# Two attentions with routed layers: the first attention's scores as three products of high and low parts, with queries and keys issued ahead and norms moved to GpSimd

## The reference

```python
x = x + attn_a(layernorm(x), w_qkv, w_out, rel_bias)   # 16 heads of 64, bias by relative position
x = x + ffn(layernorm(x), ...)                         # 8 experts, one chosen per token, times its gate
x = x + attn_b(layernorm(x), ...)                      # 16 heads, causal, low-rank keys and values
x = x + ffn(layernorm(x), ...)
```

## Time and profile before

| what | value |
|---|---|
| median of 3 runs | 665.41 us (665.12 to 666.37) |
| the profiled execution | 665.99 us, its span 664.3 us |
| granted TensorE clock, whole span | 1.000 |
| busy share: PE, PEld, DVE, ACT, POOL | 97%, 82%, 71%, 80%, 53% |
| first attention | from about 14 to 290 us |
| second attention | from about 358 to 600 us |
| second-costliest PE group, scores of both attentions (line 605) | 1024 records, 115.2 us busy, 364 ns each |

### The profile page before, as it was taken

The page is one execution under the profiler, slowest core; times in us unless marked ns, Lnnn a source line. Parts: engine busy times, 40 slices in busy tenths (PEclk is TensorE's granted clock), DMA queues, the critical chain, the costliest instruction groups (busy, mean ns, idle before and its releaser), DMA issues. The chain is left out here.

```text
span 664.3 us, 17842 instructions
## 1 busy us (share of the span) xinstructions
PE 645.2 (97%) x5406; PEld 544.9 (82%) x5406; DVE 474.9 (71%) x2147; ACT 533.3 (80%) x1776; POOL 353.9 (53%) x669
## 2 busy tenths in 40 slices
PE   6999999999999999999998999999999999999997
PEld 5778788888888788878997788878888888888997
DVE  4866767777786767988754767687868777898833
ACT  3998888889787878785765999898989898986664
POOL 4654535575546644732116545464757575472647
PEclk9999999999999999999999999999999999999999
DMA  9999989999993000035421000000000000003140
GB/s 265 276 292 283 288 204 320 292 283 288 300 285 93 26 1 2 33 98 163 128 66 41 21 1 1 2 3 9 17 14 9 14 25 2 2 34 99 54 127 21
DMA packets 86844, 74.48 MB, mean 112 GB/s; under 512 B 8001, under 2 KB 83399, under 8 KB 86496
## 3 DMA queue, kind: packets, MB, share of 16 engines
q1 hardware_dynamic: 82288, 66.24, 36.5%
q0 software_dynamic: 2848, 6.33, 3.0%
q10 hardware_dynamic: 1616, 0.79, 0.5%
HBM read 19.93 MB, written 54.00 MB: 111 GB/s over the span
## 5 line engine op out<-in xcount | busy, mean ns | idle before, releaser
L358 POOL TENSOR_SCALAR ring<-ring,rs 128x256 f32<-128x256 f32 (+1 forms) x500 | 218.1, 453 | 206.7 <-DVE rs L1255 206.3
L946 ACT ACTIVATE ring<-ring,mn 128x256 f32<-128x256 f32 (+1 forms) x512 | 243.1, 487 | 1.6 <-DVE mn L1244 1.6
L494 PE MATMUL ps<-ident,ring 128*128 128x128 f32 x896 | 121.1, 275 | 2.7 <-POOL ring L358 1.3
L605 PE MATMUL ps<-qk 64*128 64x256 f32 (+1 forms) x1024 | 115.2, 364 | 0.9 <-DVE mn L1244 0.7
L642 PE MATMUL ps<-pt,v 128*64 128x256 f32 (+1 forms) x1024 | 111.4, 359 | 0.2
L494 PEld LDWEIGHTS ps<-ident,ring 128*128 128x128 f32 x896 | 102.3, 143 | 9.1 <-POOL ring L358 2.5
L946 ACT ACTIVATION_READ_ACCUMULATOR ring<-ring,mn 128x1 f32 x512 | 103.3, 202 | 0.0
L642 PEld LDWEIGHTS ps<-pt,v 128*64 128x64 f32 x1024 | 65.6, 136 | 44.3 <-issue 13.3
L605 PEld LDWEIGHTS ps<-qk 64*128 64x128 f32 x1024 | 82.7, 187 | 18.7 <-issue 9.8
L914 ACT COPY qk<-ps 128x512 f32<-128x512 f32 x128 | 74.7, 583 | 24.1 <-PE ps L491 22.6
L1244 DVE CUSTOM_DVE_ANT_0 ring<-ps,cm 128x128 f32<-128x128 f32 (+1 forms) x256 | 73.8, 351 | 3.5 <-PE ps L605 3.5
(11 more groups left out here) (212 smaller groups left out, 1335.4 us busy)
## 6 DMA issues: line engine op xcount, KB each, us to landing
xs_scratch<-f_ys SPq DMA_DIRECT2D x16, 2064.0 KB, 23.1
yr_scratch<-f_ys SPq DMA_DIRECT2D x8, 1024.0 KB, 10.1
f_xs<-xs_scratch SPq DMA_DIRECT2D x50, 129.0 KB, 2.4
w<-in_W SPq DMA_DIRECT2D x16, 256.0 KB, 5.9
xs_scratch<-f_ys SPq DMA_DIRECT2D x2, 1677.0 KB, 21.2
yr_scratch<-f_ys SPq DMA_DIRECT2D x25, 64.0 KB, 1.5
T<-in_bias SPq DMA_DIRECT2D x2, 512.0 KB, 8.2
T<-in_bias SPq DMA_DIRECT2D x1, 1024.0 KB, 10.8
```

Of the source, the lines that this page charges most:

```text
L358: i = pool.tensor_scalar(ring[:, hh, it, 0:w], ring[:, hh, it, 0:w], rs[:, q], 1.0, ALU.mult, ALU.mult)
L494: return pe.transpose(out, src, ident[:, :])
L605: i = pe.matmul(PS[u % 2][hh][:, 256 * it:256 * it + w], qk[rows, 128 * it:128 * it + 128], qk[rows, 256:256 + w], start=True, stop=True)
L946: i = act.activation(ring[:, hh, it, 0:w], ring[:, hh, it, 0:w], ACT.Exp, bias=mn[:, q], scale=-1.0, accum_out=sm[:, q])
```

## The change

It concerns `st == 0` (the first attention) alone:

- ACT writes the queries and keys of a unit as a rounded high part (`qk_high`, float32r), and DVE, in a new operation `T`, the low part (`qk_low`), PSUM minus high part. Each has two buffers.
- The scores are three products of these parts (`S_three`), two row halves at a time.
- `QK` of an even unit from 2 on is issued in the odd step before it, behind the scores and ahead of `PV`. ACT's copy `T` of it comes between the exponentials of the two heads of unit `s - 2`; DVE's `T` of it comes between the row extremes of units `s - 1` and `s`.
- `(x - mean) * factor` ahead of the attention for sequences 1 to 7 (`pre_a2`) and ahead of gain and bias of the routed layer for sequences 0 to 6 (`post_a2`) is done by GpSimd. DVE waits for these before it overwrites the statistics.

```diff
+def norms_by_pool(st, b):
+    return st == 0 and b > 0
...
+    qk_low = at_first(low_parts, *(sb(f"qkl{i}", [128, 512], F32R, scope=low_parts) for i in range(2)))
...
+    qk_high = at_first(high_parts, *(sb(f"qkh{i}", [128, 512], F32R, scope=high_parts) for i in range(2)))
```

GpSimd:

```diff
+        def norm(dst, src, m, r, done):
+            for j in range(2):
+                i = pool.tensor_scalar(dst[:, j, :], src[:, j, :], m[:, j, 0:1], r[:, j:j + 1], ALU.subtract, ALU.mult)
+            i.then_inc(done, 1)
...
                 pool_pow(rstd, half[:, 0:2], v_var0, p_pow0, B0 + b + 1)
+                if norms_by_pool(st, b):
+                    pool.wait_ge(p_pow0, b + 1)
+                    pool.wait_ge(t_x, b)
+                    norm(a_xh, x[:, 2 * b:2 * b + 2, :], mv, rstd, p_xh)
...
             if (b := post_at(s, "a")) is not None:
-                pool.wait_ge(v_xn, B0 + b + 1)
...
+                if st == 0 and b < NB - 1:
+                    pool.wait_ge(p_pow1, b + 1)
+                    norm(xx, x[:, 2 * b:2 * b + 2, :], m2, r2[:, 2:4], p_set)
+                    set_n[0] += 1
+                    pool.wait_ge(p_set, set_n[0])
+                else:
+                    pool.wait_ge(v_xn, B0 + b + 1 - (NB - 1))
```

TensorE, in `QK` and beside `S`:

```diff
                 pe.wait_ge(a_t, U0 + u)
+                pe.wait_ge(v_t, min(U0 + u, NU))
...
+        def S_three(u):
+            high, low_ = qk_high[u % 2], qk_low[u % 2]
+            pe.wait_ge(a_t, u + 1)
+            pe.wait_ge(v_t, u + 1)
+            for hh, bank in enumerate(((1, 2), (3, 7))[u % 2]):
+                claim(bank, v_mn, 2 * u + hh + 1)
+            for it in range(2):
+                q, k_ = slice(128 * it, 128 * it + 128), slice(256, 512)
+                for n, (a, b) in enumerate(((high, high), (low_, high), (high, low_))):
+                    for hh in range(2):
+                        rows = slice(64 * hh, 64 * hh + 64)
+                        i = pe.matmul(PS[u % 2][hh][:, 256 * it:256 * it + 256], a[rows, q], b[rows, k_],
+                                      start=(n == 0), stop=(n == 2))
+            i.then_inc(t_s, 1)
```

TensorE, in its step:

```diff
-            if 0 <= s < NU:
+            if 0 <= s < NU and not (st == 0 and s and s % 2 == 0):
                 QK(s)
...
                 S(s - 1)
                 S(s)
+                if st == 0 and s + 1 < NU:
+                    QK(s + 1)
```

ACT, in `T`:

```diff
-            act.copy(a_qk[(U0 + u) % 2][:, :], PT_[:, :]).then_inc(a_t, 1)
+            if st == 0:
+                act_high(qk_high[u % 2][:, :], PT_[:, :], a_t)
```

ACT, in its step:

```diff
+            early = st == 0 and s % 2 and 1 <= s < NU - 1
+            if early and s < 2:
+                T(s + 1)
             if 2 <= s < NU + 2:
-                expo(s - 2, (0, 1) if s % 2 or s == NU else (0,))
+                expo(s - 2, (0, 1) if (s % 2 and not early) or s == NU else (0,))
+                if early:
+                    T(s + 1)
+                    expo(s - 2, (1,))
```

DVE:

```diff
+        def T(u):
+            if u >= 2:
+                dve.wait_ge(t_s, u - 1)
+            low(qk_low[u % 2][:, :], PT_[:, :], qk_high[u % 2][:, :], a_t, u + 1, v_t)
...
         def post_a2(b):
+            if st == 0 and b < NB - 1:
+                return
```

DVE, in its step; in an odd step the first addition stands ahead of the update and `TR`, the second between `S(s - 1)` and `S(s)`:

```diff
+            if st == 0 and 0 <= s < NU and (s % 2 or s == 0):
+                T(s)
...
+                if st == 0 and s + 1 < NU:
+                    T(s + 1)
```

More of the change, by code:

```diff
@@ L213, in build, with at_first @@
     f_tok = sb("f_tok", [128, NF], U32)
+    def at_first(scope, *made):
+        scope.close()
+        return made
+    low_parts = ExitStack()
+    qk_low = at_first(low_parts, *(sb(f"qkl{i}", [128, 512], F32R, scope=low_parts) for i in range(2)))
     f_xt = [sb(f"f_xt{i}", [128, 512]) for i in range(2)]
@@ L221, in build @@
     f_sub = sb("f_sub", [128, 4, NE])
-    def at_first(scope, *made):
-        scope.close()
-        return made
     base = ExitStack()
@@ L234, in build @@
     a_pt = [sb(f"pt{i}", [128, 2, 512], scope=base) for i in range(2)]
+    high_parts = ExitStack()
+    qk_high = at_first(high_parts, *(sb(f"qkh{i}", [128, 512], F32R, scope=high_parts) for i in range(2)))
     a_qk = [sb(f"qk{i}", [128, 512], scope=base) for i in range(2)]
@@ L270, in build @@
     p_set, p_nrm, p_xn, p_T = sem("p_set"), sem("p_nrm"), sem("p_xn"), sem("p_T")
-    p_pow0, p_pow1 = sem("p_pow0"), sem("p_pow1")
+    p_pow0, p_pow1, p_xh = sem("p_pow0"), sem("p_pow1"), sem("p_xh")
     t_m, t_wv, t_wo = sem("t_m"), sem("t_wv"), sem("t_wo")
@@ L284, in build @@
     v_m, v_wv, v_wo, v_kd = (sem(n) for n in ("v_m", "v_wv", "v_wo", "v_kd"))
+    v_t = sem("v_t")
     v_x, v_l, v_mn, v_rs, v_nrm, v_pt1, v_o = (
@@ L527, in pre_b @@
             PX = spare(("x", B0 + b), v_x, B0 + b + 1, None if B0 + b else 7)
-            pe.wait_ge(v_xh, B0 + b + 1)
+            if norms_by_pool(st, b):
+                pe.wait_ge(p_xh, b)
+            else:
+                pe.wait_ge(v_xh, b + 2 if st else 1)
             for j in range(2):
@@ L594, in first_queries @@
             three(PT_[:, 0:256], wqkh[:, 0:128], wqkl[:, 0:128], a_xth[0][:, :], a_xtl[0][:, :])
+        def S_three(u):
[12 more added lines that the diff above has]
+            i.then_inc(t_s, 1)
         def S(u):
+            if st == 0:
+                S_three(u)
+                return
             qk = a_qk[(U0 + u) % 2]
@@ L913, in T @@
                 act.wait_ge(t_s, U0 + u - 1)
-            act.copy(a_qk[(U0 + u) % 2][:, :], PT_[:, :]).then_inc(a_t, 1)
+            if st == 0:
+                act_high(qk_high[u % 2][:, :], PT_[:, :], a_t)
+            else:
+                act.copy(a_qk[(U0 + u) % 2][:, :], PT_[:, :]).then_inc(a_t, 1)
         def values(b, n):
@@ L1198, in pre_a @@
         def pre_a(b):
+            if norms_by_pool(st, b - 1):
+                dve.wait_ge(p_xh, b - 1)
+            if st and b == 0:
+                dve.wait_ge(p_xh, NB - 1)
             come = d_yt[2 * b:2 * b + 2] if st else (d_x[min(b, 2)], None)
@@ L1284, in out_last @@
             dve.wait_ge(v_res, B0 + b + 1)
+            if st == 0:
+                dve.wait_ge(p_xn, b)
             norm_a(xx, s2, m2, r2, v_var1)
@@ L1294, in sums @@
             dve.wait_ge(v_res, B0 + b + 1)
+            if st == 0 and b:
+                dve.wait_ge(p_xn, b)
             norm_a(x[:, 2 * b:2 * b + 2, :], s2, m2, r2, v_var1)
```

## The result

The changed kernel takes **688.6 us** (median of 4 runs, 688.46 to 691.57) beside 665.89 us for the kernel before (4 runs, 665.12 to 668.48): a ratio of 1.035 [1.033, 1.038], 22.7 us slower. The sign of the forecast holds, and its mechanism does in the steady pairs; the size does not, above all at the start: 13.8 us were forecast, and 688.6 lies 0.6 beyond the range's upper end, 688 (for the lower end the forecast gives 671 in one place and 660 in another). The profiled execution took 688.62 us.

What follows compares the result with a forecast made beforehand. TensorE bounded the kernel; after the change a path through ACT, DVE and GpSimd would set 8.3 us pairs. Pair, placement and start terms sum to 13.8: 665.99 + 13.8 - 0.6 = 679.2 us, range 671 to 688 (elsewhere 660 to 688).

Steps and rivals of the forecast that it cites:

- The mechanism: First attention pairs: DVE's wait for ACT's copy delays minima, reciprocal, GpSimd's scaling and TensorE's transposes; 8.3 us; chance 0.62.
- TensorE stays the bound: Rival, first attention: the path through the other engines is under some 7.8 us; total about 661 us; chance 0.22.
- The scores: TensorE's score block of a pair takes 1.60 us instead of 1.93, a gain of 0.33, loads side by side.
- rival of serial loads: TensorE's score loads of two row halves do not run side by side; 1.4 us more, 724 in all; chance 0.07.
- The extra change of shape: Moving QK between S and PV adds one change of TensorE's array shape per pair, +0.19 us.
- The sums' pair: Pair with the step of the sums: DVE's update, copy and statistics lengthen the path to 9.0 us instead of 8.3.
- the projection's: Pair holding the output projection: TensorE's own sum, 11.01 us, a change of -0.14, seven times.
- placement: DVE's placement chain stands ahead of the odd unit's low part; TensorE's S(o) waits 1.35 us, three times.
- The plain pairs: Pairs with neither sums nor projection: the path through DVE and GpSimd sums to 8.29, taken as 8.3 us.
- The start: DVE's low parts of units 1 and 2 queue late: 1.8 us (0.7 to 2.5), plus 0.3 for a first pair.
- The end: Last pair of the first attention: +0.6 us, counted with the sums' pairs.
- The norms: Two 128x128 operations per sequence moved from DVE to GpSimd: 0.4 us each, costed at nothing; uncovered, some 8 more.

Runs made afterwards that it cites:

- experiment 5: Changed kernel plus an unread 128x512 DVE addition in 24 pairs, between the next even unit's low part and S(o)'s minima; +37.0 us against the kernel before.
- experiment 6: Changed kernel plus an unread 128x512 DVE addition in 24 pairs, behind the copy of the transposes in the even step; +27.2 us against the kernel before.
- experiment 4: Changed kernel with plain float32 scores and no low parts, QK still early, norms still on GpSimd; +6.6 us against the kernel before.
- Experiment 13: Changed kernel with float32 scores and no low parts in the first sequence (units 0 to 7); +17.7 us against the kernel before.
- experiment 12: Changed kernel with three-product scores only in even units from 8, QK in its own step, low part mostly behind the kept one; 680.17 us beside 680.92 before.
- experiment 3: Changed kernel with the norms back on DVE; +22.2 us against the kernel before.
- experiment 8: Changed kernel with e+2's low part behind minima and reciprocal, unit 1's ahead of the weights' at the start, placement one step later; +21.7 us against before.

## Why the prediction was right in kind and short in size

**The mechanism** held step by step: "TensorE would wait for GpSimd 0.2 to 0.6 us per pair" (0.53 above), DVE idle 0.70 before the low part where 0.7 was named, and the minima of S(o) queued behind it. Experiments 5 and 6 show that this place is the path of plain and sums' pairs. The "TensorE stays the bound" rival turned on a path below 7.8 us; it measures 8.48.

**The scores.** 1.60 us forecast, 1.61 measured (the rest of 0.20 in it belongs to 8 pairs at 0.216, not to the 7 named). The rival of serial loads is refuted: two halves' products stand in one record pair and the pairs are 0.12 apart, so float32r loads of two row halves run side by side. By the columns rule of the Trainium skill ("TensorE: Matmul & The Clock Gate", LDWEIGHTS) alone 24 loads would take 2.6 us by estimate. The trace, with 1.61 us for the block, goes with its section on row and column tiling, by which loads overlap where row groups differ. **The extra change of shape**, 0.19: 0.18 to 0.20 by experiment 4.

**The sums' pair**, 9.0 against 9.00 (its terms add up to 9.07); **the projection's**, 11.01 against 11.04; **placement**, 1.35 us of wait against 1.42 and 1.41 (12.46 and 12.45 less 11.04) and, as the last projection was 0.22 shorter before too, 1.15. The sizes are right, 8.5 of the 13.8. There is some luck in them: DVE's time before the placement is written as 8.6 where its terms give 8.73, and the projection's pair was taken as TensorE's own without asking for the chain beside it, which experiment 5 shows to be just as long.

**The plain pairs** are the first term of the sum that was too small, by a little, many times: 8.48 for 8.29. The three terms are "to S 0.97" (1.03: TensorE restarts after a hole), the copy and its handover to DVE (0.70 for 0.58 and "0.03") and the step from the reciprocal to GpSimd (0.26 instead of 0.08 and 0.10). These make 0.23, the rest -0.04; 14 pairs and the three before placements at 8.65 make 3.1 us.

**The start** was the large miss, "1.8 by estimate (0.7 to 2.5)" and 0.3 for one of the first pairs, against 6.4 measured. The step of the prediction that failed is "once more the same plus a wait": I counted DVE's delay, and not that TensorE would stand still for 2.9 us and then run at 1.2 GHz, nor that QK(3) waits for the low part of unit 2, as both use the one PSUM bank. "QK(o) comes ... over 3 us, for a copy and a low part of 1.3: nothing" was argued for the steady stage and not for the start, where DVE is behind. Experiment 13 gets 5.0 us of it back in the runs. How much of it is waiting and how much the lower clock was not separated.

**The end**, 0.6 against 1.4. In the changed kernel the second half of the last transposes waits 0.70 for DVE's copy, behind the kept low part and a norm. In experiments 4 and 12 the last pair is about as long (8.88, 8.62), with no low parts of queries and keys or fewer of them, and in 4 the same wait of 0.70 stands; so they are not needed for it. In 4 the reciprocal waits 1.02 us for ACT's exponentials, in 12 QK(63) waits 1.16 for the low part of unit 62. Which of these dominates after the change was not separated: the cause at the end stays open.

**The norms** were mis-sized (0.79 for 0.4), and cost nothing in sum, as forecast (experiment 3).

Start +4.3, plain +3.1, end +0.8, placement and projection +0.2, 0.3 behind the stage: together 8.7, and these are, but for rounding, the 8.9 us between the rise forecast (13.8) and measured (22.7). The times themselves, 679.2 and 688.6, are 9.4 apart, since the kernel before has its median 0.5 higher in the later runs.

## What to carry to other kernels

Before an operation is put on an in-order engine, ask what it waits for and who is queued behind it: 0.6 us of DVE work cost 0.6 us per pair in one place and 0.02 in another, on an engine that is idle a quarter of the span. Such a share is a mean: in the stretches where DVE was full, at the placements, the same work cost time off the path too. A saving on the engine that was the bound (here 0.3 us a pair) is worth something only as long as no other chain is longer than what is left. Here the other chain had 7.1 us of 7.86 before and 8.48 after, because the change itself put an operation and a wait on it. So compute that chain first, with the handovers measured and not guessed. Look at the first pairs apart: queues that keep up in the steady stage start full there, and a hole in TensorE costs again through its clock.

## What was not expected of the hardware

- GpSimd's norm of 128x128 with two scalars per row takes 0.79 us (777 to 819 ns), while its 128x256 scaling with one takes 0.46 (1.84 / 4), and DVE's norm 0.34.
- With one more change of the array between full and row halves and back, pairs of four kinds grow by 0.18 to 0.20 us each (experiment 4).
- A hole of 2.9 us in TensorE was followed by products 0.22 us apart instead of 0.12, from 17.2 to about 23 us. Shorter holes did it too, and not each time: of two holes of 1.8 us in experiment 8 and two of 1.65 in experiment 6, the granted clock fell behind one of each.
- The kernel before took 665.9 us on one chip and 677.7 to 681.6 on others. There is no trace of the kernel before from the other chips. But where versions have the same program in a stretch, the traces put the difference behind the first attention: its steady pairs are equal to 0.03 us (9.00, 8.49, 11.04 in experiments 3 and 13 as after), the second attention takes 238 to 242 us there and 235 here. Why was not studied.
